# Row maxima turned by TensorE, an order of its own for each engine, and normalisations on ScalarE, in a three-stage layer kernel

## The reference

```
x = x + time_mix(layernorm(x))
x = x + ffn(layernorm(x))

time_mix:  k = x Wk^T;  r = v = x Wr^T          # per token
  state (a, b, p) per channel, scanned over the tokens:
    q  = max(p, u + k);  y = (e^(p-q) a + e^(u+k-q) v) / (e^(p-q) b + e^(u+k-q))
    p' = max(p + w, k);  a' = e^(p+w-p') a + e^(k-p') v;  b' = e^(p+w-p') b + e^(k-p')
  out = (sigmoid(r) * y) Wo^T

ffn: h = rmsnorm(x);  q = h Wq + bq;  k, v = split((h Wdown + bdown) Wup + bup)
  16 heads of 32 channels; the softmax runs over the heads of one token
  x = x + out Wo + bo;  h2 = rmsnorm(x);  gate = softmax(h2 Wg + bg) over 8 experts
  result = x + sum over e of gate[e] * (h2 We[e])
```

## Time and profile before

| | |
|---|---|
| median of three runs | 3332.1 us |
| the profiled execution | 3332.17 us, span 3330.3 |
| TensorE busy (matmuls) | 2887.2 us, 87% |
| VectorE busy | 2476.6 us, 74% |
| ScalarE busy | 956.6 us, 29% |
| GpSimd busy | 686.1 us, 21% |
| chain that ended last | TensorE 62%, VectorE 23%, issue 7%, SyncE's queue 5%, DMA 2% |
| transfers over 16 engines | 16.4% of the span, mostly under 512 B |
| mean granted TensorE clock | 0.941 |

### The profile page before, as it was taken

One profiled execution on the slowest core, in us unless ns is written; L12 is line 12 of the kernel. 1 busy time (PEld: TensorE's weight loads), 2 busy tenths in 40 slices (PEclk: granted clock), 3 DMA queues, 4 the chain that ended last, 5 costly groups with the idle time before them and its releaser, 6 DMA issues.

```text
span 3330.3 us, 53600 instructions
## 1 busy us (share of the span) xinstructions
PE 2887.2 (87%) x18864; PEld 1791.2 (54%) x18864; DVE 2476.6 (74%) x4548; ACT 956.6 (29%) x1823; POOL 686.1 (21%) x745
## 2 busy tenths in 40 slices
PE   2359999998888989989998898999889998999889
PEld 2235555554555655555564555555555555555544
DVE  5797777778777768777777777768777777877753
ACT  2243232322332322322331332232233232232320
POOL 0111222212122212222221222221222221212210
PEclk9669999999999999999999999999999999999999
DMA  6011111101111101111111111111111110111110
GB/s 192 15 24 20 33 33 26 30 24 33 20 33 27 33 20 33 20 33 26 33 27 26 20 33 30 29 26 27 27 26 33 27 33 20 32 21 33 26 20 13
DMA packets 588333, 102.96 MB, mean 31 GB/s; under 512 B 556562, under 2 KB 556690, under 8 KB 588050
## 3 DMA queue, kind: packets, MB, share of 16 engines
q1 hardware_dynamic: 588068, 99.40, 16.4%
HBM read 48.49 MB, written 16.78 MB: 20 GB/s over the span
## 4 chain that ended last, share of the span: by engine, by line
PE 62%; DVE 23%; issue 7%; SPq 5%; DMA 2%; ACT 0%; POOL 0%; DVEq 0%; ACTq 0%; POOLq 0%
PE bank L1049 49%; PE bank L1201 6%; DVE mcol L954 4%; SPq L424 4%; DVE zz L865 3%; PE bank L1079 3%; DVE ks L943 3%; DVE wkv L839 2%; PE bank L1191 2%; DMA qs<-m 2%; DVE acc L1028 1%; DVE wkv L827 1%; PE bank L1165 1%; DVE ht L935 1%; DVE zz L832 1%
## 5 line engine op out<-in xcount | busy, mean ns | idle before, releaser
L1049 PE MATMUL bank<-w_e,h2t 128*128 128x512 f16 x6144 | 1479.4, 398 | 19.1 <-DVE acc L1028 19.1
L1049 PEld LDWEIGHTS bank<-w_e,h2t 128*128 128x128 f16 x6144 | 617.9, 103 | 757.5 <-issue 123.1
L1028 DVE SCALAR_TENSOR_TENSOR acc<-bank,gates,acc 128x512 f32<-128x512 f32 x512 | 373.6, 737 | 164.7 <-PE bank L1049 163.6
L1201 PEld LDWEIGHTS bank<-vp,pr 128*128 128x128 f32 x2048 | 263.9, 197 | 24.0 <-DVE hrow L970 3.9
L1201 PE MATMUL bank<-vp,pr 128*128 128x33 f32 x2048 | 259.7, 275 | 3.8 <-ACT pr L608 2.7
L608 ACT ACTIVATE pr<-bank,col 128x512 f32<-128x512 f32 x256 | 171.9, 685 | 316.1 <-PE bank L1191 315.7
L865 DVE RECIPROCAL zz<-zz 128x256 f32<-128x256 f32 x128 | 219.1, 1733 | 46.8 <-POOL zz L462 46.8
L1049 PE MATMUL bank<-w_o,xo 128*128 128x512 f16 x768 | 174.3, 384 | 58.8 <-DVE xo L799 58.8
L455 POOL TENSOR_TENSOR e<-wkv 128x512 f32<-128x512 f32 x64 | 72.1, 1127 | 645.6 <-DVE wkv L827 645.6
L1191 PE MATMUL bank<-qs,ks 106*128 106x128 f16 x1024 | 104.5, 236 | 113.9 <-DMA qs<-m 113.9
L1182 PE MATMUL bank<-ks,qs 104*128 104x128 f16 x1024 | 90.8, 231 | 125.7 <-DMA ks<-k 65.7
(11 more groups left out here) (177 smaller groups left out, 3918.1 us busy)
## 6 DMA issues: line engine op xcount, KB each, us to landing
qs<-qo SPq DMA_DIRECT2D x384, 64.0 KB, 3.0
xk<-in_attn_x SPq DMA_DIRECT2D x32, 512.0 KB, 3.9
x<-in_attn_x SPq DMA_DIRECT2D x32, 512.0 KB, 3.6
result<-acc SPq DMA_DIRECT2D x32, 512.0 KB, 2.8
ks<-k SPq DMA_DIRECT2D x128, 64.0 KB, 3.0
w_e<-in_ffn_We SPq DMA_DIRECT2D x7, 1024.0 KB, 13.8
qs<-m SPq DMA_DIRECT2D x256, 2.0 KB, 1.7
qs<-in_attn_Wk SPq DMA_DIRECT2D x1, 1024.0 KB, 5.5
```

What stands on the lines that cost most here:

```text
L1028: V.scalar_tensor_tensor(out=acc[:, s, :], in0=moe_bank[u % 2][:, :], scalar=gates[:, s, e:e + 1], in1=acc[:, s, :], op0=ALU.mult, op1=ALU ...
L1049: ins = nc.tensor.matmul(dst, left(a), right(b), start=(n == 0), stop=(n == last))
L1201: ins = nc.tensor.matmul(att_bank[ATT_BANK["PV", k]][:, n * (HD + 1):(n + 1) * (HD + 1)], pr[:, k % 2, n * P:(n + 1) * P], vp[:, 4 * k + n ...
```

## The change

Every engine gets an order of its own. The row maxima are turned by one transpose on TensorE and written in two transfers. Differences and clippings of the recurrence are rearranged: VectorE makes one difference d = k - p of the running maximum before the step, z is made of it by one add-and-minimum per channel block, and both decays follow from it on ScalarE as exp(-relu(d + e^w)) and exp(-relu(-d - e^w)), `ecol` and `wcol` holding e^w and -e^w. The denominator's and numerator's sums are made by GpSimd. The normalisations and the attention's values are ScalarE's Identity or Copy with scale and bias; VectorE only makes the bias -mean * rstd. `ZMAX` goes from 87 to 64.

```diff
-ORDER = [ ... one list ... ]
+PE_ORDER = [
+    ("mix_turn", 0), ("moe", 0), ("moe", 1), ("att_turn", 0), ("mix_k", 0), ("att_latent", 0), ("att_q", 0),
+    ("att_up", 0), ("mix_v", 0), ("moe", 2), ("moe", 3), ("moe", 4), ("att_max", 0), ("att_max", 1), ("moe", 5),
+    ("att_max", 2), ("moe", 6), ("att_max", 3), ("moe", 7), ("att_m", 0), ("moe", 8), ("moe", 9), ("att_scores", 0),
+    ("att_scores", 1), ("att_probs", 0), ("att_scores", 2), ("att_probs", 1), ("att_scores", 3), ("att_probs", 2),
+    ("att_scores", 4), ("att_probs", 3), ("att_scores", 5), ("moe", 10), ("att_probs", 4), ("att_scores", 6),
+    ("att_probs", 5), ("att_scores", 7), ("moe", 11), ("att_probs", 6), ("att_probs", 7), ("moe", 12), ("moe", 13),
+    ("att_project", 0), ("moe", 14), ("moe", 15), ("att_turn2", 0), ("mix_project", 0), ("att_gate", 0),
+]
+DVE_ORDER = [
+    ("att_stats", 0), ("att_norm", 0), ("mix_turn", 0), ("moe_gate", 0), ("att_turn", 0), ("att_latent", 0),
+    ("mix_decay", 0), ("moe", 0), ("moe", 1), ("att_stack", 0), ("moe", 2), ("att_vt", 0), ("moe", 3), ("mix_sum", 0),
+    ("mix_value", 0), ("att_max", 0), ("moe", 4), ("att_max", 1), ("moe", 5), ("att_max", 2), ("att_max", 3),
+    ("moe", 6), ("mix_scan", 0), ("att_m", 0), ("moe", 7), ("mix_rec", 0), ("mix_rec", 1), ("mix_gate", 0),
+    ("att_probs", 0), ("att_probs", 1), ("moe", 8), ("moe", 9), ("att_probs", 2), ("att_probs", 3), ("mix_split", 0),
+    ("mix_decay", 1), ("moe", 10), ("att_probs", 4), ("att_probs", 5), ("moe", 11), ("att_probs", 6), ("mix_sum", 1),
+    ("att_probs", 7), ("att_back", 0), ("mix_value", 1), ("mix_scan", 1), ("mix_rec", 2), ("moe", 12), ("moe", 13),
+    ("att_project", 0), ("mix_rec", 3), ("mix_gate", 1), ("moe", 14), ("mix_split", 1), ("pre_stats", 0), ("moe", 15),
+    ("att_turn2", 0), ("pre_norm", 0), ("mix_project", 0),
+]
+ACT_ORDER = [
+    ("mix_turn", 0), ("att_norm", 0), ("moe_gate", 0), ("moe", 0), ("att_turn", 0), ("mix_k", 0), ("moe", 1),
+    ("att_latent", 0), ("att_q", 0), ("att_up", 0), ("mix_v", 0), ("moe", 2), ("moe", 3), ("mix_exp", 0), ("moe", 4),
+    ("att_rest", 0), ("moe", 5), ("moe", 6), ("moe", 7), ("moe", 8), ("mix_num", 0), ("att_scores", 0),
+    ("att_scores", 1), ("att_scores", 2), ("att_scores", 3), ("moe", 9), ("mix_split", 0), ("att_scores", 4),
+    ("att_scores", 5), ("moe", 10), ("att_scores", 6), ("moe", 11), ("att_scores", 7), ("mix_exp", 1), ("moe", 12),
+    ("moe", 13), ("att_back", 0), ("mix_num", 1), ("moe", 14), ("moe", 15), ("att_square", 0), ("att_norm2", 0),
+    ("mix_split", 1), ("att_turn2", 0), ("pre_norm", 0),
+]
+POOL_ORDER = [
+    ("att_stats", 0), ("moe_acc", 0), ("att_q", 0), ("att_up", 0), ("mix_sum", 0), ("mix_num", 0), ("mix_sum", 1),
+    ("moe", 15), ("mix_num", 1), ("att_rest", 0), ("att_square", 0), ("pre_stats", 0),
+]
+SP_ORDER = [ ("mix_k", 0), ("att_up", 0), ("att_m", 0), ("pre_load", 0), ("moe_store", 0) ]
...
             def att_m(t, _):                                   # SyncE
-                    for f in range(F):
-                        sp.dma_start(qs[SCAN_ROWS + l:SCAN_ROWS + l + 1, :, f, :], m16[f * G:(f + 1) * G, l, :]).then_inc(m_in.sem, 16)
+                    sp.dma_start(qs[SCAN_ROWS + l:SCAN_ROWS + l + 1, :, :, :].rearrange("a g f x -> a g (f x)"), m16[:, l, :]).then_inc(m_in.sem, 16)
...
+            def att_m(t, _):                                   # TensorE
+                pe.wait_ge(*att_dve.done(t, "smax"))
+                nc.tensor.transpose(att_bank[TURNED_M][0:G, 0:P], mcol[:, :], ident[:, :]).then_inc(att_pe.sem, 1)
...
             def att_m(t, _):                                   # VectorE
-                V.transpose(mturn[:, :], mcol[:, :]).then_inc(att_dve.sem, 1)
+                dve.wait_ge(*att_pe.done(t, "MT0"))
+                V.tensor_scalar(m16[:, 0, :], turned_m, -2.0 ** -14, None, ALU.mult).then_inc(att_dve.sem, 1)
...
-            def mix_decay(t, h):                               # GpSimd: two differences, gone
             def mix_sum(t, h):                                 # GpSimd
-                pool.wait_ge(*mix_dve.done(t, f"b_{h}"))
-                pool.wait_ge(*mix_act.done(t, f"r_{h}"))
+                pool.wait_ge(*mix_dve.done(t, f"zv_{h}"))
                 nc.gpsimd.tensor_tensor(zz[:, :, :], wkv[:, 2, :, 0:T], zz[:, :, :], ALU.add).then_inc(mix_pool.sem, 1)
+            def mix_num(t, h):
+                pool.wait_ge(*mix_dve.done(t, f"a_{h}"))
+                nc.gpsimd.tensor_tensor(ev[:, :, :], wkv[:, 1, :, 0:T], ev[:, :, :], ALU.add).then_inc(mix_pool.sem, 1)
...
             def mix_exp(t, h):                                 # ScalarE
+                act.wait_ge(*mix_dve.done(t, f"dd_{h}"))
+                for c in range(HF):
+                    nc.scalar.activation(e1[:, c, :], e2[:, c, :], ACT.Relu, bias=ecol[...]).then_inc(mix_act.sem, 1)
+                act.wait_ge(*mix_dve.done(t, f"z_{h}"))
+                act.wait_ge(*mix_act.done(t, f"ra_{h}"))
+                for c in range(HF):
+                    nc.scalar.activation(e2[:, c, :], e2[:, c, :], ACT.Relu, bias=wcol[...], scale=-1.0).then_inc(mix_act.sem, 1)
+                nc.scalar.activation(e1[:, :, :], e1[:, :, :], ACT.Exp, scale=-1.0).then_inc(mix_act.sem, 1)
+                nc.scalar.activation(e2[:, :, :], e2[:, :, :], ACT.Exp, scale=-1.0).then_inc(mix_act.sem, 1)
+                nc.scalar.activation(zz[:, :, :], zz[:, :, :], ACT.Exp).then_inc(mix_act.sem, 1)
...
             def mix_decay(t, h):                               # VectorE, behind the running maximum
+                V.tensor_tensor(e2[:, :, :], k32[...], wkv[:, 0, :, 0:T], ALU.subtract).then_inc(mix_dve.sem, 1)
                 for c in range(HF):
-                    V.scalar_tensor_tensor(out=zz[:, c, :], in0=k32[...], scalar=ucol[...], in1=wkv[:, 0, c, 0:T], ...)
-                V.tensor_scalar(zz[:, :, :], zz[:, :, :], ZMAX, None, ALU.min).then_inc(mix_dve.sem, 1)
+                    V.tensor_scalar(zz[:, c, :], e2[:, c, :], ucol[...], ZMAX, ALU.add, ALU.min).then_inc(mix_dve.sem, 1)
+            def mix_value(t, h):                               # VectorE
+                V.tensor_tensor(ev[:, :, :], zz[:, :, :], vh, ALU.mult).then_inc(mix_dve.sem, 1)
+                dve.wait_ge(*mix_dve.done(t, f"b_{h}"))
+                V.tensor_tensor(e2[:, :, :], e2[:, :, :], vh, ALU.mult).then_inc(mix_dve.sem, 1)
...
             def mix_gate(t, h):                                # VectorE
+                V.tensor_tensor(ev[:, :, :], ev[:, :, :], zz[:, :, :], ALU.mult).then_inc(mix_dve.sem, 1)
-                ... a product, a sum and the gate; mix_num's product and difference are gone too
+                V.scalar_tensor_tensor(out=ev[:, :, :], in0=e1[:, :, :], scalar=1.0, in1=ev[:, :, :], ...)
...
+            def att_norm2(t, _):                               # ScalarE; pre_norm, att_norm, att_rest alike, with Identity and a bias
+                act.wait_ge(*att_pool.done(t, "rms"))
+                for s in range(SUB):
+                    nc.scalar.activation(h_rows[:, s, :], x2[:, s, :], ACT.Copy, scale=rs3[:, s:s + 1]).then_inc(att_act.sem, 1)
...
             def att_up(t, _):                                  # ScalarE, behind the keys; VectorE's is gone
+                for b in range(CB):
+                    act.wait_ge(*att_pe.done(t, f"V{b // 2}"))
+                    nc.scalar.activation(va32[:, :, b, :], att_bank[...], ACT.Identity, bias=bvcol[:, b:b + 1], scale=colof["vv"])
```

More of the change, by code:

```diff
@@ L304, in att_reader, with pipeline @@
             return {"T": (att_dve, "h_lo", k), "D": (att_act, "c", 0), "Q": (att_act, "q", 4 * k + 2),
-                    "K": (att_act, "k", 4 * k + 2), "V": (att_dve, "v", 2 * k + 1),
-                    "M": (att_dve, "smax", k), "S": (att_act, "ex", k), "PV": (att_dve, "norm", 2 * k + 1),
+                    "K": (att_act, "k", 4 * k + 2), "V": (att_act, "v", 2 * k + 1),
+                    "M": (att_dve, "m_lo", 0) if k == 7 else (att_dve, "smax", k), "S": (att_act, "ex", k), "PV": (att_dve, "norm", 2 * k + 1),
                     "O": (att_dve, "x2", k), "T2": (att_dve, "h2_lo", k),
                     "G": (gate_dve, "gl", 0)}[use]
-        def pipeline(eng, steps, split=None, between=None):
+        def pipeline(eng, order, steps, split=None, between=None):
             def iteration(i, par, chunk):
@@ L323, in iteration @@
                     tiles["moe"] = Tile(i - 2, par, chunk - 1)
-                for name, k in ORDER:
+                for name, k in order:
                     stage_name = name.split("_")[0]
@@ L529, in _, with pre_norm @@
                 split_block(n)
+            def pre_norm(t, _):
+                act.wait_ge(*pre_dve.done(t, "shift"))
+                for s in range(SUB):
+                    nc.scalar.activation(xk_rows[:, s, :], xk_rows[:, s, :], ACT.Identity, bias=nb1[:, s:s + 1], scale=rs1[:, s:s + 1])\
+                        .then_inc(pre_act.sem, 1)
             def mix_turn(t, _):
```

(17 more changed lines are left out.)

173 lines of the change are left out of this document (66 added, 107 removed).

## The result

Four runs of the changed kernel gave 3252.39 to 3258.98 us, median 3258.5, against 3332.1 before: 0.9774 of it (95% interval 0.9757 to 0.9791), 73.6 us less. The forecast was 172 us less.

What follows compares the result with a forecast made beforehand. TensorE sets the pace: 84.6 us of own work plus holes make 90.2, with clock 91.2, against 96.4. Saving 5.2 us in thirty iterations (156) and 16 at the ends gives 3332 - 172 = 3160 us, range 3092 to 3262.

Steps and rivals of the forecast that it cites:

- late chain: Rival: ScalarE's instructions before half 1's sums delay transpose, projection, `moe 14` and norm; 2.6 us an iteration, 3240 us; chance 0.20.
- The maxima's path: Last row maximum to scores: one transpose, two transfers, about 3.9 us from turned maxima to scores, covered by two products.
- The holes that remain: TensorE's waits left: stacked keys 2.7 us, first exponential 0.9, alternation 0.3, projection 0.1, `moe 14` 0.9, norm 0.1, low half 0.6.
- The collision of GpSimd's sum and the scans: VectorE's scans meet GpSimd's sum: 0 to 1.26 us, taken as 1.0, making `moe 14` wait 0.9.
- VectorE as cover: VectorE loses about 11 to 12 of 75 us an iteration; cover, not gain, until its late chain near 1590.
- The normalisations that I called hidden but for 0.1: Layer norms moved to ScalarE: hidden behind TensorE's products, except 0.1 us at the norm before the experts.
- The clock: TensorE's low-clock stretches: two of 1.3 us each per iteration before; after, between 0 and 1.3, taken as 1.0.
- more than one stretch at the low clock per iteration: Sign, listed beforehand, that would show the prediction wrong: TensorE at the low clock more than once in an iteration.
- The reference iteration: Kernel before: four iterations together 390.7 us, 97.7 each; 96.4 without the loop's edge, which costs about 2.6 every second iteration.
- The ends: First two iterations and next to last: 4 to 8 us gained each, 16 together; last iteration unchanged.
- everything fits: Rival: VectorE's late chain finds its port free and the clock holds; 7.1 us per iteration gained, 3100 us; chance 0.17.

Runs made afterwards that it cites:

- the run with eight: Changed kernel with one part undone, the turned row maxima sent in eight transfers again instead of two: 3383.1 us (1.0155).
- the run with the accumulations first: Changed kernel with product 10 and `att_rest` moved forward, ten filling matmuls, four iterations per loop body, VectorE's accumulations 12 and 13 before the scans: 3097.6 us (0.9295).
- The best version run: Changed kernel, product 10 and `att_rest` forward, accumulations 12 and 13 before scans, ten fillings at keys, two at first exponential, eight iterations per body: 3076.4 us (0.9225).

## Why the prediction was wrong

The direction was right and the size was not: 73.6 us instead of 172. That 3258.5 lies just inside the stated range (3092 to 3262) is luck: the upper end was set by the rival "late chain", whose mechanism didn't occur. Step by step:

- **The maxima's path**: right. No wait of the transfers, which by the run with eight land about 1.9 us before their use (1.3 forecast). The maxima on VectorE no longer hold TensorE up.
- **The holes that remain**: right. Stacked keys 2.4 to 2.75 us (2.7), first exponential 0.56 idle, 0.72 from start to start (0.9), `moe 14` 0.50 (0.9), low half 0.48 (0.6), projection and norm none (0.1 each), none in the alternation of scores and probabilities (0.3). Forgotten were the 0.3 us before the second half of the values: counted as lost before, they stand there after the change too.
- **The collision of GpSimd's sum and the scans**: right. The two scans take 2.28 us at 1567.48 and 1.39 elsewhere, 0.9 (1.0), and the run with the accumulations first, where no scan is longer than 0.75, shows the cause.
- **VectorE as cover**: right in its busy time, 64 us of an iteration (63) and ScalarE's 39 (39). The normalisations that I called hidden but for 0.1 are worth 45 us, 1.5 an iteration, because VectorE's late chain would carry them.
- **The clock: the step that failed.** "Before, two stretches at the low level cost 1.3 us each per iteration. After, one hole of 2.7 us is left ... Between 0 and 1.3; I take 1.0." The forecast had the clock give back 1.6 us an iteration (2.6 to 1.0). It took 1.1 more instead (4.2 to 5.3). I tied the low clock to long waits, so I counted one stretch where there are two or three: behind the wait for keys (3.2 us of low time), at the scores and probabilities (5.5), where TensorE is busy nearly all the time with narrow matmuls, and at the loop's edge (2.0). The prediction had itself named "more than one stretch at the low clock per iteration" as a sign of being wrong. Before, the low time at the scores (4.1) stood at and behind the wait of 2.8 us for the maxima's transfers, which is gone. What took its place was made by the change: `PE_ORDER` has 5.8 us of scores and probabilities in a row, while the common order had a product between every two pairs, as the rows of before behind the earlier trace rows show:

```profile
1582.89 0.39 PE L1191 MATMUL bank<-qs,ks 106*128 106x128 f16 x4
1583.12 1.03 PE L1201 MATMUL bank<-vp,pr 128*128 128x33 f32 x8
1583.99 0.39 PE L1191 MATMUL bank<-qs,ks 106*128 106x128 f16 x4
1584.21 2.75 PE L1049 MATMUL bank<-w_e,h2t 128*128 128x512 f16 x12
```

  Moving one product gives 68 us back.
- **The reference iteration.** Four iterations at 97.7 us stood for the kernel before. The mean of the loop is 98.8, and its clock costs 4.2 us, where I counted 2.6. With 98.8 as the start the forecast would have been larger still, so this error hid part of the other.
- **The ends.** 16 us were taken for the first iterations and the last ones. They gave 4.5: the first iteration with all stages starts at 244.2 us in both traces.

The account for one iteration of the loop: forecast 84.6 of own work and 5.6 of holes, 90.2, with 1.0 of clock and 1.3 for the edge 92.5. Measured: 85.4 of own work (busy time at the full clock) and 4.6 of waits, 90.0 (-0.2); clock 5.2 by the busy time (+4.2); wait at the edge 40.5 / 26 = 1.6 (+0.3); sum 96.8. About 1.0 of this clock stands around the edge; the forecast had it in its 1.3, so that the clock inside the iteration is 4.2 against 1.0 and the edge in all 2.6 against 1.3.

The rival "late chain" named 3240 us and would have come close by number. Its mechanism is refuted: there are no table loads in the loop, TensorE's waits for VectorE and ScalarE are 0.3 to 0.6 us each but for two single ones, and filling matmuls, which take nothing off VectorE or ScalarE, made the kernel faster by 56 us. The best version run, with changes of its own at the edge and on VectorE, went below the rival "everything fits" (3100).

What stays open is when exactly the clock falls at the scores. It does so in all 26 iterations of the loop, but not in the iterations at 244 and at 2944 us, which have the same order, the same 5.7 us of scores and probabilities and a shorter wait for the keys (1.5 and 1.7 us). That wait alone doesn't decide it either: with the wait filled, 4.3 us of low time remained at the scores.

Not tried: the shorter recurrence by itself, and the separate orders by themselves.

## What to carry to other kernels

When an edit moves wide matmuls away from narrow ones, look at the granted clock of the new sequence as if it were a wait: here a TensorE that was busy 95% of the time still lost 2 to 3 us per iteration. An iteration that happens to have no low stretch, such as the first one with all stages, tells what TensorE's own work is worth; compare its waits with the loop's before its length is taken for the schedule's. The mean over the loop tells what the clock takes. And a path that is made shorter pays only if the next engine's queue has nothing waiting in front of the work that it releases: with one common order for all engines, 62 of the 73 us taken off that wait came back as a wait for ScalarE.

## What the runs showed of the hardware

- The granted clock can fall where TensorE hardly waits. From 1546.1 to 1550.7 us it does scores and probabilities back to back, busy 9.45 us of the 10 up to 1550, and the product behind them runs partly at the low level (4.25 us, 0.76 granted from 1550 to 1557); with a wide matmul in front of each group of scores the low time there went from 4.3 us an iteration to 0. The same rows at 294.8 to 300.4 us ran at the full clock, so the narrow matmuls are not enough by themselves.
- A loop's edge costs TensorE 3.4 us of waiting on average (40.5 us in 12, the longest 4.0), and more by the clock behind it: seven edges fewer saved 72 us, 12 of them in a shorter wait for the stacked keys.
- ScalarE's Identity with scale and bias from SBUF takes 806 ns for 512 elements, Square 631. I had used the latter. These rows are groups of the changed kernel, 1500 to 1888 us (busy us, mean ns, idle before):

```profile
L480 POOL TENSOR_TENSOR zz<-wkv,zz 128x512 f32<-128x512 f32 x8 | 13.1, 1642 | 140.3 <-DVE ev L906 140.3
...
L607 ACT ACTIVATE hrow<-x,nb,rs 128x512 f32<-128x512 f32 x8 | 6.1, 806 | 7.7 <-DVE nb L961 7.7
```

The Trainium skill ("ScalarE: Activation LUTs", section "What ACT_TABLE_LOAD costs") gives 186 ns and 0.833 per element with immediates and some 93 ns more for each pointer operand. For two of them that makes an estimate of 799, and the trace's 806 agrees.
- GpSimd's sum, 1264 ns on average before, takes 1642 after. It starts at 1566.92 us, while VectorE's product of two SBUF tensors runs (1566.76 to 1567.45), and VectorE's first scan behind that product starts at 1567.48, while the sum still runs: it takes 1634 ns, the seven other scans of the iteration 719 to 744. With the scans moved away the sum still takes 1646 ns and no scan more than 754, so the product holds the sum up and the sum holds the scans up. The exclusive port pair of the Trainium skill ("SBUF — State Buffer", section "SBUF: two separate sides") agrees with both in kind: each time the instruction that starts second is the longer one.
